# First block in another order: W1's product by inner halves, the low-rank rows turned in halves, GpSimd's splits elsewhere; in the last block the scores' shift ahead of a copy

## Chip, cores and metric

One core of a Trainium2 chip runs the whole program. The metric is the device time of one execution in microseconds (us).

## What is computed

x is 2 x 1024 x 256, the context 2 x 64 x 192, all float32. Four residual steps follow each other, each on a layer norm of x:

```
x = x + L0_xattn(_layernorm(x), ctx)   # 16 heads of 16; then relu(out @ W1 + b1) @ W2 + b2, W1 256 x 512
x = x + L0_ffn(_layernorm(x))          # for each of 8 experts: gate * (relu(x @ wi.T + bi + (x @ A_e.T) @ B_e.T) @ wo.T + bo)
x = x + L1_xattn(_layernorm(x), ctx)   # one head, width 256, softmax over 64 keys
x = x + L1_ffn(_layernorm(x))          # x @ weight.T + pooled @ disha
```

The gate of an expert is how often it is among the top two logits, times the sum of the two largest softmax values. So only two experts count for a row, and only their low-rank terms (A_e, B_e) differ.

## The kernel before

The 2048 rows are cut into 8 blocks of 256 rows (T = 256, two tiles of 128). Each block goes through stage a (first attention, W1, W2), stage f (experts), stage c (second attention and last product). The program writes out the order of each engine's work by hand: `opening()` is block 0's stage a and the start of its stage f together with all loads and weight preparation; `body(a, f, c, h)` runs seven times and mixes stage a of block a, stage f of block a-1, stage c of block a-2 and the queries of block a+1; `drain` and `end` finish the last two blocks. Engines are tied only by semaphores (`wait_ge`, `then_inc`).

Precision: most products are made three times in fp32r. Each operand is split in a high part (ScalarE copies the float32 value to fp32r) and a low part (VectorE or GpSimd subtracts the high part); the passes are high x high, low x high, high x low. Names end in _h and _l. For weights, `high_weights(n)` (ScalarE) and `low_weights(n)` (VectorE, counted in `lo_w`, or GpSimd, counted in `lo_wp`) do this once, in the opening: wq, w1, w2, wi in two halves, ga (A and the gate's weights, 128 x 272), lb (B), wo.

Names for the steps spoken of:
- `filler` (PE, L771): a product of zeros, used by nothing.
- `transposes(1, 0)` (L362) turn the normalised block 0; `values` (L685) are the first attention's values; `a_queries(0)` (L347) the queries; `a_row_scores` (L402) and `row_max` (VectorE, L1317) give each head's maximum; `first_scores` (L447), `first_exps` (ScalarE, L963), `first_attend` (L487, L488) the attention of block 0.
- `query_means` (L670, 4 products of float32) and a copy to `wqm` (VectorE, L1721): column means of Wq, used in block 1 and later.
- `a_hidden` (W1's product, into psS), ScalarE's `hidden` (relu, L1024) and `hidden_high` (L1029), `hidden_low` (GpSimd L1776 for the first half, VectorE L1665 for the second), `a_out` (W2's product, into psP), VectorE's `first_residual` (xmid, L1365) and `norm_stats(2, 0)`, GpSimd's `scale(2, 0)` (rs, L1759: the inverse root), ScalarE's `normalise(2, 0)` (xn, L970), `transposes(2, 0)`, `f_gate` (ga), VectorE's `experts` (am: the masked low-rank rows), `f_lora_transposes` (L543), ScalarE's `lora_high`, VectorE's `lora_low` (at_l, L1407), `f_first` (L567).
- `fold_turn`, `fold_means` (L642, L651), `constant_parts`, `constant_row` (L693, L700), `values1` (L685), `folded_keys` (L723, L726): preparation of stage c and of the experts' constant.
- `indicators(b)` (GpSimd, L1885): one 16 x 1024 table of each batch entry; the second is used from block 4 on.
- Last block (`end`): `end_turn` (L733) turns a tile, `passes` (L347) make its scores and linear part in one bank, ScalarE's `linear_part` (L1106) copies the linear part out, VectorE (L1519) shifts and scales the scores, ScalarE (L1110) takes the exponentials.

## Time and profile before

| what | value |
|---|---|
| median of 3 runs | 309.53 us (309.51 to 312.08) |
| the profiled execution's own time | 309.51 us |
| its span, first to last instruction | 307.5 us |
| mean granted TensorE clock | 0.994 |
| PE, DVE, ACT, POOL busy | 293.0, 256.8, 172.6, 161.2 us |
| chain that ended last | PE 83%, DVE 8%, ACT 3%, DMA 2%, POOL 1% |

Engines: PE is the matrix engine, PEld its weight loads, DVE is VectorE, ACT ScalarE, POOL GpSimd, SP the engine that issues DMAs. A float32 product leaves two records on PE, an fp32r product one. Records of PE overlap by their modelled ends, so starts are compared with starts. "Idle before" names what the engine waited for.

### The profile page before, as it was taken

The numbers are of one execution on the slowest core, as the hardware profiler recorded it, in microseconds if no ns is written. First come the engines' busy times: TensorE is split into PE (matmuls) and PEld (weight loads), VectorE is DVE, ScalarE is ACT, GpSimd is POOL, SyncE is SP. The second block draws the span as 40 slices with busy tenths as digits, with TensorE's granted clock in tenths as the row PEclk, the third lists the DMA queues.
The fourth block names the chain that finished last, engine by engine and source line by source line (L and its number), as shares of the span: only waits on it lengthen the run. The fifth ranks groups of instructions, "written<-read, shape, count | busy, mean of one in ns | idle before, by whom it ended". The sixth has DMA issues, their size and how long they took to land.

```text
span 307.5 us, 6696 instructions
## 1 busy us (share of the span) xinstructions
PE 293.0 (95%) x2548; PEld 272.3 (89%) x2548; DVE 256.8 (84%) x706; ACT 172.6 (56%) x359; POOL 161.2 (52%) x156
## 2 busy tenths in 40 slices
PE   7789998999999999999999999999999999999972
PEld 5559887999989998999999998999899998999971
DVE  3798988979899988998799889988899879755666
ACT  3548388564667267535846565826853584434521
POOL 2845665894085705581476318560659044803562
PEclk9999999999999999999999999999999999999997
DMA  7993320014021320133013301122023000000001
GB/s 234 395 388 105 73 68 2 0 45 128 2 19 39 71 100 2 24 89 114 2 19 77 96 35 19 44 71 91 3 29 94 36 0 2 0 36 1 2 34 34
DMA packets 15903, 20.18 MB, mean 66 GB/s; under 512 B 2912, under 2 KB 11872, under 8 KB 15616
## 3 DMA queue, kind: packets, MB, share of 16 engines
q1 hardware_dynamic: 14176, 16.19, 19.3%
q10 hardware_dynamic: 1696, 3.57, 3.2%
q8 instruction: 20, 0.33, 0.5%
q14 instruction: 11, 0.09, 0.2%
HBM read 11.62 MB, written 2.63 MB: 46 GB/s over the span
## 4 chain that ended last, share of the span: by engine, by line
PE 83%; DVE 8%; ACT 3%; DMA 2%; issue 2%; POOL 1%; SPq 0%; POOLq 0%; DVEq 0%
PE psI L567 13%; PE psP L347 13%; PE psI L338 12%; PE psI L347 12%; PE psS L347 7%; PE psT L338 4%; PE psP L502 2%; DMA kv<-in_kv 2%; PE psS L475 2%; PE psT L634 2%; PE psT L362 2%; PE psP L742 1%; PE psT L605 1%; PE psP L543 1%; ACT hs L1024 1%
## 5 line engine op out<-in xcount | busy, mean ns | idle before, releaser
L1759 POOL TENSOR_TENSOR rs<-ve,mhalf 128x2 f32<-128x2 f32 x30 | 22.0, 733 | 86.0 <-DVE ve L1285 86.0
L1782 POOL TENSOR_TENSOR hid_l<-r,hid_h 128x512 fp32r<-128x512 f32 x32 | 40.9, 1291 | 16.0 <-ACT hid_h L1049 16.0
L567 PE MATMUL psI<-at_h,lb_h 128*128 128x256 f32 x120 | 34.6, 289 | 0.8 <-DVE at_l L1407 0.8
L567 PE MATMUL psI<-at_h,lb_l 128*128 128x256 f32 x120 | 33.9, 282 | 0.0
L567 PE MATMUL psI<-at_l,lb_h 128*128 128x256 f32 x120 | 33.7, 281 | 0.0
L1415 DVE SCALAR_TENSOR_TENSOR r<-psI,nbi,r 128x256 f32<-128x256 f32 x60 | 26.1, 477 | 6.4 <-PE psI L567 6.4
L1776 POOL TENSOR_TENSOR hs_l<-hs,hs_h 128x512 fp32r<-128x512 f32 x15 | 19.6, 1310 | 20.6 <-ACT hs_h L1029 19.7
L970 ACT ACTIVATE xn<-xmid,nmr,rs 128x256 f32<-128x256 f32 x16 | 8.8, 595 | 35.8 <-POOL nmr L1763 35.8
L1044 ACT ACTIVATE r<-psI,first 128x256 f32<-128x256 f32 x60 | 25.0, 472 | 4.3 <-PE psI L567 4.3
L567 PEld LDWEIGHTS psI<-at_h,lb_h 128*128 128x128 f32 x120 | 22.6, 188 | 4.3 <-ACT r L1044 2.9
L1049 ACT ACTIVATE hid_h<-r 128x512 fp32r<-128x512 f32 x32 | 20.0, 628 | 11.0 <-DVE r L1415 10.8
L338 PE MATMUL psI<-xtf_h,wi_h 128*128 128x256 f32 x120 | 26.0, 298 | 0.0
L338 PE MATMUL psI<-xtf_h,wi_l 128*128 128x256 f32 x120 | 24.1, 283 | 0.0
L338 PE MATMUL psI<-xtf_l,wi_h 128*128 128x256 f32 x120 | 24.0, 282 | 0.0
L1008 ACT ACTIVATE ex<-psS 128x512 f32<-128x512 f32 x28 | 15.9, 599 | 13.6 <-PE psS L475 13.6
L567 PEld LDWEIGHTS psI<-at_h,lb_l 128*128 128x128 f32 x120 | 22.6, 189 | 0.0
L567 PEld LDWEIGHTS psI<-at_l,lb_h 128*128 128x128 f32 x120 | 22.6, 188 | 0.0
L338 PEld LDWEIGHTS psI<-xtf_h,wi_h 128*128 128x128 f32 x120 | 18.4, 189 | 2.2 <-issue 2.2
L338 PEld LDWEIGHTS psI<-xtf_l,wi_h 128*128 128x128 f32 x120 | 18.5, 189 | 0.0
L338 PEld LDWEIGHTS psI<-xtf_h,wi_l 128*128 128x128 f32 x120 | 18.5, 189 | 0.0
L1018 ACT ACTIVATE oa_h<-o 128x256 fp32r<-128x256 f32 x16 | 6.7, 418 | 18.2 <-DVE o L1358 17.3
L1767 POOL TENSOR_TENSOR oa_l<-o,oa_h 128x256 fp32r<-128x256 f32 x15 | 11.9, 809 | 9.4 <-ACT oa_h L1018 9.4
(344 smaller groups left out, 910.8 us busy)
## 6 DMA issues: line engine op xcount, KB each, us to landing
stack<-qu_h SPq DMA_DIRECT2D x56, 64.0 KB, 2.1
xin<-in_x SPq DMA_DIRECT2D x8, 256.0 KB, 2.8
stack<-qu_l SPq DMA_DIRECT2D x28, 64.0 KB, 2.0
out<-x ACTq DMA_DIRECT2D x7, 256.0 KB, 2.0
xn<-in_xt SPq DMA_DIRECT2D x5, 256.0 KB, 3.0
raw_w<-in_w ACTq DMA_DIRECT2D x2, 512.0 KB, 8.4
raw_wi<-in_wi SPq DMA_DIRECT2D x1, 1024.0 KB, 9.6
raw_wo<-in_wo SPq DMA_DIRECT2D x1, 1024.0 KB, 12.4
```

Source lines behind the costliest of these rows:

```text
L338: last = mm(out, lhs(a, c), rhs(b, c), start=start and q == 0 and k == 0, stop=stop and q == 2 and k == n - 1, **kw)
L347: last = mm(out, lhs(a, c), rhs(b, c), start=start and (a, b) == pairs[0] and i == 0 and k == 0, stop=stop and k == len(chunks) - 1, skip_ ...
L567: last = mm(bank[:, k * T:(k + 1) * T], (WH, WL)[x]["lb"][:, 0, f * P:(f + 1) * P], AT[y][:, which, :], start=False, stop=q == 2, skip_gro ...
L970: A(XN[j][:, t, :], src[:, t, :], ACT.Identity, scale=lnst[j][4][:, t:t + 1], bias=lnst[j][5][:, t:t + 1]).then_inc(S(f"ln{j}_xh"), 1)
L1008: A(EX[:, 2 * d:2 * d + 2, :], S_(d % 2).rearrange("p (k n) -> p k n", k=2), ACT.Exp, scale=SCALE).then_inc(S("ex"), 1)
L1044: last = A(R1[:, f, :], bank[:, k * T:(k + 1) * T], ACT.Relu, bias=cols[:, BI + f:BI + f + 1])
L1049: A(HH[:, 2 * u:2 * u + 2, :], R1[:, 2 * u:2 * u + 2, :], ACT.Identity).then_inc(S("hidh"), 1)
L1415: last = V.scalar_tensor_tensor(out=R1[:, f, :], in0=bank[:, k * T:(k + 1) * T], scalar=nbi[:, f:f + 1], in1=R1[:, f, :], op0=MAX, op1=ADD)
L1759: G_.tensor_tensor(rs[:, :], ve[:, :], mhalf[:, :], ALU.pow).then_inc(S(f"ln{j}_rs"), 1)
L1767: G_.tensor_tensor(OA[1][:, m, :], O32[:, m, :], as32(OA[0][:, m, :]), ALU.subtract).then_inc(S("ol"), 1)
L1776: G_.tensor_tensor(HS[1][:, two, :], HS32[:, two, :], as32(HS[0][:, two, :]), ALU.subtract).then_inc(S("hsl"), 1)
L1782: G_.tensor_tensor(HL[:, two, :], R1[:, two, :], as32(HH[:, two, :]), ALU.subtract).then_inc(S("hidl"), 1)
```

## The change

In `opening` PE makes the queries' means in two halves between products of block 0 and no longer after the attention, into another bank; four fillers more stand in it, at other places; the transposes of block 0 stand ahead of the values. W1's product of block 0 (`first_hidden`) takes the first inner half (m = 0) of all four output parts, then `values1(0)`, then the second inner half, so that it starts on the first half of the attention's output. Row scores of block 1 take the small form of later blocks. The queries of block 1 go to psP and no longer to psI, `constant_parts` move ahead and to psP, `fold_turn` and `fold_means` into the first body behind `f_first(0, 0)`. The low-rank rows of block 0 are turned, split and used in two halves. In the first body the low pass of `f_out(0, 0)` stands ahead of the next block's transposes. The small splits ga_l and wo_l change engine or place, `indicators(1)` moves to the second body with f = 1, the copy to gnum is gone from all blocks. In `end` the second tile's turn stands between the first tile's passes, the shift waits for the product and not for the copy, and the copies stand behind the exponentials.

PE, the first 13 us of the program, before and now (zeros is a filler, a_60 the keys, kv_61 the values, wq,avg the means, kb,qu_h the row scores):

```order
L678 MATMUL psI<-a_60 128x128 x4
L685 MATMUL psS<-kv_61 128x256 x2
L362 MATMUL psT<-first,xn 128x128 x4
L771 MATMUL psP<-zeros 128x256 x2
L347 MATMUL psP<-xta_h,wq_h 128x256 x4
L347 MATMUL psP<-xta_h,wq_l 128x256 x4
L347 MATMUL psP<-xta_l,wq_h 128x256 x4
L771 MATMUL psP<-zeros 128x256
L402 MATMUL psS<-kb,qu_h 128x512 x2
```

```order
L709 MATMUL psI<-a_60 128x128 x4
L802 MATMUL psP<-zeros 128x256 x3
L362 MATMUL psT<-first,xn 128x128 x4
L716 MATMUL psS<-kv_61 128x256 x2
L347 MATMUL psP<-xta_h,wq_h 128x256 x4
L347 MATMUL psP<-xta_h,wq_l 128x256 x4
L347 MATMUL psP<-xta_l,wq_h 128x256 x4
L700 MATMUL psT<-wq_h,avg 128x256 x2
L398 MATMUL psS<-kb,qu_h 128x512 x2
L398 MATMUL psI<-kb,qu_h 128x512 x2
L700 MATMUL psT<-wq_l,avg 128x256 x2
L802 MATMUL psP<-zeros 128x256
```

The means stand on both sides of the row scores, and the transposes stand ahead of the values.

PE, from the end of block 0's attention to block 1's queries, before and now (oa_h and oa_l are the attention's output, w_h and w_l are W1, xta the next block's input):

```order
L670 MATMUL psS<-wq_h,avg 128x256 x2
L670 MATMUL psS<-wq_l,avg 128x256 x2
L362 MATMUL psI<-first,xn 128x128 x4
L685 MATMUL psT<-kv_61 128x256 x2
L707 MATMUL psT<-a_60,kv_62 128x128 x4
L347 MATMUL psS<-oa_h,w_h 128x256 x4
L347 MATMUL psS<-oa_h,w_l 128x256 x4
L347 MATMUL psS<-oa_l,w_h 128x256 x4
L347 MATMUL psS<-oa_h,w_h 128x256 x4
L347 MATMUL psS<-oa_h,w_l 128x256 x4
L347 MATMUL psS<-oa_l,w_h 128x256 x4
L347 MATMUL psI<-xta_h,wq_h 128x256 x4
```

```order
L716 MATMUL psT<-kv_61 128x256 x2
L802 MATMUL psI<-zeros 128x256
L362 MATMUL psI<-first,xn 128x128 x4
L740 MATMUL psT<-a_60,kv_62 128x128 x4
L347 MATMUL psS<-oa_h,w_h 128x256 x2
L347 MATMUL psS<-oa_h,w_l 128x256 x2
L347 MATMUL psS<-oa_h,w_h 128x256 x2
L347 MATMUL psS<-oa_h,w_l 128x256 x2
L347 MATMUL psS<-oa_l,w_h 128x256 x4
L716 MATMUL psI<-kv_62,kv_61 128x256 x2
L347 MATMUL psS<-oa_h,w_h 128x256 x2
```

The means are gone here, and W1's product, 24 instructions in both, now has 12 on the first inner half, the values of the second attention, and 12 on the second inner half.

GpSimd from W1's product on, before and now (hsl counts finished low halves of the hidden values, rs is the inverse root):

```order
L1767 TENSOR_TENSOR oa_l<-o,oa_h 128x256 [waits oh]
L1892 TENSOR_TENSOR kb<-kt_h,first 128x512 [waits kt0_h]
L1892 TENSOR_TENSOR kb<-kt_h,first 128x512
L1776 TENSOR_TENSOR hs_l<-hs_59,hs_h 128x512 [waits hsh]
L1882 TENSOR_TENSOR wi_l<-raw_wi,wi_h 128x1024 [waits hi_w]
L1759 TENSOR_TENSOR rs<-ve,mhalf 128x2 [waits ln2_ve]
L1763 TENSOR_TENSOR nmr<-nm,rs 128x2 [waits ln2_rs]
L1799 TENSOR_TENSOR xr<-xin_50,kept 128x512 [waits x_in,x1]
L1882 TENSOR_TENSOR lb_l<-raw_lb,lb_h 128x1024 [waits hi_w]
L1922 TENSOR_TENSOR gw<-gw,late 128x2x256 [waits ld_late,ld_wc]
L1882 TENSOR_TENSOR wo_l<-raw_wo,wo_h 128x1024 [waits hi_w]
```

```order
L1825 TENSOR_TENSOR oa_l<-o,oa_h 128x256 [waits oh]
L1834 TENSOR_TENSOR hs_l<-hs_59,hs_h 128x512 [waits hsh]
L1946 TENSOR_TENSOR wi_l<-raw_wi,wi_h 128x1024 [waits hi_w,hsl]
L1946 TENSOR_TENSOR ga_l<-raw_ga,ga_h 128x272 [waits hi_w]
L1817 TENSOR_TENSOR rs<-ve,mhalf 128x2 [waits ln2_ve]
L1821 TENSOR_TENSOR nmr<-nm,rs 128x2 [waits ln2_rs]
L1955 TENSOR_TENSOR kb<-kt_h,first 128x512 x2
L1946 TENSOR_TENSOR lb_l<-raw_lb,lb_h 128x1024 [waits hi_w]
L1857 TENSOR_TENSOR xr<-xin_50,kept 128x512 [waits x_in,x1]
L1986 TENSOR_TENSOR gw<-gw,late 128x2x256 [waits ld_late,ld_wc]
L1817 TENSOR_TENSOR rs<-ve,mhalf 128x2 [waits ln1_ve]
L1821 TENSOR_TENSOR nmr<-nm,rs 128x2 [waits ln1_rs]
```

The table kb and lb_l stand behind block 0's rs now, ga_l (VectorE's before) ahead of it, and wo_l behind block 2's rs.

```diff
+            def first_hidden():
+
+                pe.wait_ge(S("lo_w"), 2)
+                parts = [[(S_(u)[:, k * T:(k + 1) * T], w("w1", (2 * u + k) * P), x_of(OA)) for k in range(2)]
+                         for u in range(NDH)]
+                for m in range(KC):
+                    pe.wait_ge(S("oh"), m + 1)
+                    for u in range(NDH):
+                        passes(parts[u], [m], ((0, 0), (1, 0)), m == 0, False)
+                    pe.wait_ge(S("ol"), m + 1)
+                    for u in range(NDH):
+                        last = passes(parts[u], [m], ((0, 1),), False, m == KC - 1)
+                        if m == KC - 1:
+                            last.then_inc(S("hs_ps"), 1)
+                    if m == 0:
+                        values1(0)
+
...
-                end_turn(b, 1)
...
+                def upper(t):
                     pe.wait_ge(S("ln3_h"), b + t + 1)
-                    passes(parts, range(KC), ((0, 0), (0, 1)), True, False)
+                    passes([(SCORES[t][:, 0:SY], x_of(XTC, t * P, P), folded_weights(b))], range(KC), ((0, 0), (0, 1)),
+                           True, False)
+
+                def lower(t):
                     pe.wait_ge(S("ln3_l"), b + t + 1)
-                    passes(parts, range(KC), ((1, 0),), False, True).then_inc(S("sc1_ps"), 1)
+                    passes([(SCORES[t][:, 0:SY], x_of(XTC, t * P, P), folded_weights(b))], range(KC), ((1, 0),),
+                           False, True).then_inc(S("sc1_ps"), 1)
+
+                upper(0)
+                end_turn(b, 1)
+                lower(0)
+                upper(1)
+                lower(1)
...
-                if A_:
-                    a_scores(a, 0)
-                    a_scores(a, 1)
-                if F_:
+                if f == 0:
+                    first_lora_transposes(0)
+                    first_lora_transposes(1)
+                a_scores(a, 0)
+                a_scores(a, 1)
+                if f > 0:
                     f_lora_transposes(f)
-                if f == 0:
-                    fold_means()
                 if C_:
                     c_scores(c, 0)
                     c_scores(c, 1)
                 if F_:
                     f_first(f, 0)
+                    if f == 0:
+                        fold_turn()
+                        fold_means()
                     if A_:
                         a_scores(a, 2)
                     f_first(f, 1)
@@ -867,7 +910,7 @@
                     a_row_scores(h, 1)
                 if F_:
                     f_out(f, 1, low=False)
-                if F_ and C_:
+                if F_:
                     f_out(f, 0, high=False)
...
-                if F_ and not C_:
-                    f_out(f, 0, high=False)
...
+                pe.wait_ge(S("ld_first"), 16)
+                filler(P_(1), 3)
+                transposes(1, 0, T_(1))
                 pe.wait_ge(S("ld_kv0"), 16)
                 values(S_(0)[:, 0:D], kv0, 0).then_inc(S("v0_ps"), 1)
-                pe.wait_ge(S("ld_first"), 16)
-                transposes(1, 0, T_(1))
-                filler(P_(1), 2)
                 a_queries(0)
-                filler(P_(1), 1)
+                query_means(0)
                 pe.wait_ge(S("v0"), 1)
                 a_row_scores(0, 0)
                 pe.wait_ge(S("kt0_l"), KC)
                 a_row_scores(0, 1, I_)
+                query_means(1)
+                filler(P_(1), 1)
                 first_scores(((0, 0), (1, 0)))
                 first_max_transposes()
                 first_scores(((0, 1),))
                 first_scores_less_maxima()
+                filler(I_(1), 2)
                 first_attend(0)
                 first_attend(1)
-                query_means()
+                values(T_(1)[:, 0:D], kv0, 1).then_inc(S("v0_ps"), 1)
+                filler(I_(1), 1)
                 transposes(1, 1, I_(0))
-                values(T_(1)[:, 0:D], kv0, 1).then_inc(S("v0_ps"), 1)
                 keys1()
-                a_hidden(0, 0)
-                pe.wait_ge(S("centred"), 2)
-                a_hidden(0, 1)
-                a_queries(1, I_(1))
+                first_hidden()
+                a_queries(1)
                 a_out(0, 0)
                 a_out(0, 1)
-                pe.wait_ge(S("kt1"), 1)
-                pe.wait_ge(S("v0"), BATCH)
-                a_row_scores(1, 0, T_)
-                a_row_scores(1, 1, S_)
-                values1()
+                row_scores(1)
+                constant_parts()
+                values1(1)
                 folded_keys()
                 pe.wait_ge(S("mx"), 2 * NT - 1)
                 transposes(2, 0, T_(1))
-                pe.wait_ge(S("mx"), 2 * NT)
-                constant_parts()
+                folded_biases()
                 a_max_transposes(1)
+                pe.wait_ge(S("crow"), 1)
                 f_gate(0, 1)
+                constant_row()
                 pe.wait_ge(S("gb"), 1)
                 f_base(0, 0)
-                constant_row()
                 pe.wait_ge(S("v1"), 1)
                 f_base(0, 1)
-                fold_turn()
...
                 def linear_part(t):
-                    act.wait_ge(S("sc1_ps"), b * NT + t + 1)
+                    act.wait_ge(S("sc1b"), b * NT + t + 1)
                     A(YB[b // BPB][:, t, :], SCORES[t][:, at:at + D], ACT.Identity).then_inc(S("y"), 1)
 
                 def weights(t):
@@ -1117,12 +1160,12 @@
                 for t in range(NT):
                     tile_high(3, b, t, XTC)
                 store(b - 1)
-                linear_part(0)
-                linear_part(1)
                 weights(0)
                 turned(0)
                 weights(1)
                 turned(1)
+                linear_part(0)
+                linear_part(1)
...
+                act.wait_ge(S("centred"), 1)
+                A(wqm[:, :], T_(0)[:, 0:D], ACT.Identity).then_inc(S("centred"), 1)
                 first_maxima()
                 first_exps(0)
                 first_exps(1)
                 normalise(1, 1, x_of_block(1))
                 attended(0, 0)
+                high(1, 1, XTA, I_(0))
                 high_weights("wi", 0, 2)
-                high(1, 1, XTA, I_(0))
                 attended(0, 1)
...
+                high_weights("wo")
+                act.wait_ge(S("crow_ps"), 1)
+                A(y[:, 0:D], P_(0)[:, 0:D], ACT.Identity).then_inc(S("crow"), 1)
                 normalise(2, 0, XMID)
                 high(2, 0, XTF, T_(1))
-                act.wait_ge(S("crow_ps"), 1)
-                A(y[:, 0:D], S_(1)[:, 0:D], ACT.Identity).then_inc(S("crow"), 1)
...
-                high_weights("wo")
...
-                V.tensor_copy(gnum[:, :], lg3[:, :, 0])
...
-                    dve.wait_ge(S("y"), b * NT + t + 1)
+                    dve.wait_ge(S("sc1_ps"), b * NT + t + 1)
...
-                if F_:
+                if f == 0:
+                    first_lora_low(0)
+                    constant()
+                    first_lora_low(1)
+                    gates(0)
+                    dve.wait_ge(S("nbi"), 1)
+                else:
                     lora_low(f)
...
@@ -1698,46 +1761,41 @@
...
+                low(1, 0, XTA, T_(1))
...
-                low(1, 0, XTA, T_(1))
+                masked_values(0, S_(0))
                 dve.wait_ge(S("kt0_l"), KC)
                 diagonal(kd_l, kt0_l, "kd_l")
-                dve.wait_ge(S("ld_vrows"), 16)
-                first_values(0, S_(0)[:, 0:D])
                 row_max(0, 0)
                 row_max(0, 1, psI)
                 queries_low(0)
-                low_weights("w1")
+                first_values(0)
                 dve.wait_ge(S("x_in"), 32)
                 dve.wait_ge(S("ln1_xh"), NT)
                 norm_stats(1, 1, x_of_block(1))
+                low_weights("w1")
                 V.tensor_scalar(nbi[:, :], cols[:, BI:BI + NFF], -1.0, None, MULT).then_inc(S("nbi"), 1)
                 first_attended(0)
                 first_attended(1)
-                dve.wait_ge(S("centred"), 1)
-                V.tensor_copy(wqm[:, :], S_(1)[:, 0:D]).then_inc(S("centred"), 1)
                 attended_low(0, 1)
                 low(1, 1, XTA, I_(0))
-                first_values(1, T_(1)[:, 0:D])
+                low_weights("wi", 1, 2)
+                masked_values(1, T_(1))
+                first_values(1)
                 keys_of_second()
-                low_weights("wi", 1, 2)
                 hidden_low(0, 1)
                 queries_low(1)
-                low_weights("ga")
                 first_residual(0)
                 dve.wait_ge(S("x1"), 1)
                 norm_stats(2, 0, XMID)
-                row_max(1, 0, psT)
-                row_max(1, 1)
+                heads_max(1, 1, psT)
+                heads_max(1, 0, psS)
+                values_of_second()
                 low(2, 0, XTF, T_(1))
-                values_of_second()
                 experts(0)
-                constant()
...
+                if f == 0:
+                    low_weights("wo", 0, 2)
...
+                if f == 1:
+                    pool.wait_ge(S("ol"), (a + 1) * KC)
+                    indicators(1)
+                    pool.wait_ge(S("tables"), 4)
...
@@ -1902,26 +1965,26 @@
                 pool.wait_ge(S("ld_first"), 16)
                 pool.wait_ge(S("ln1_nmr"), 1)
                 indicators(0)
-                indicators(1)
+                pool.wait_ge(S("tables"), 1)
                 pool.wait_ge(S("ld_vrows"), 16)
                 G_.tensor_copy(heads[:, :], heads32).then_inc(S("tables"), 1)
-                low_weights("w2", 0, 1)
                 pool.wait_ge(S("ld_kept"), 16)
                 residual(0)
+                low_weights("w2", 0, 1)
                 scale(1, 1)
                 attended_low(0, 0)
-                pool.wait_ge(S("kt0_h"), KC)
+                hidden_low(0, 0)
+                pool.wait_ge(S("hsl"), NDH)
+                low_weights("wi", 0, 2)
+                low_weights("ga", 0, 1)
+                scale(2, 0)
                 second_row_keys()
-                hidden_low(0, 0)
-                low_weights("wi", 0, 2)
-                scale(2, 0)
+                low_weights("lb", 0, 1)
                 residual(1)
-                low_weights("lb", 0, 1)
                 pool.wait_ge(S("ld_wc"), 16)
                 pool.wait_ge(S("ld_late"), 16)
                 G_.tensor_tensor(GWR[:, :, KEYS:KEYS + D], GWR[:, :, KEYS:KEYS + D],
                                  late[:, D:2 * D].unsqueeze(1).broadcast_to([P, KC, D]), ALU.add).then_inc(S("wc_sum"), 1)
-                low_weights("wo", 0, 2)
```

## Rows read from the trace of the kernel before

**Rows 1.** Windows view, columns as named in its head (us; PEclk of 1.00 full).

```profile
0.00:20.00 20.00, 14.38 (x106) 10.68 (x108) 13.10 (x32) 8.75 (x18) 10.91 (x11) 1.00 0.93 332
20.00:60.00 40.00, 38.87 (x330) 34.33 (x323) 34.68 (x77) 27.55 (x55) 23.92 (x22) 1.00 0.26 77
60.00:290.00 230.00, 229.58 (x2056) 218.82 (x2055) 196.86 (x557) 132.16 (x279) 117.40 (x114) 1.00 0.18 43
290.00:307.50 17.50, 10.15 (x69) 8.44 (x67) 12.17 (x42) 4.09 (x11) 8.96 (x11) 0.89 0.08 30
```

**Rows 2.** PE timeline to 22 us: start, duration, engine, line, operation, tiles, records, idle before.

```profile
4.89 2.05 PE L678 MATMUL psI<-a 96*128 96x128 f32 x8
8.50 1.13 PE L685 MATMUL psS<-kv 96*128 96x256 f32 x4 [1.56 <-DMA kv<-in_kv]
...
12.34 0.59 PE L771 MATMUL psP<-zeros 128*128 128x256 f32 x2
13.47 0.70 PE L402 MATMUL psS<-kb,qu_h 128*128 128x512 f32 x2 [0.54 <-issue]
...
15.49 0.39 PE L447 MATMUL psS<-qu_h,kd_h 32*128 32x256 f32 x2 [0.85 <-DVE mx L1317]
...
19.27 0.63 PE L487 MATMUL psP<-ex,v0z 128*32 128x256 f32 x4 [0.84 <-ACT ex L963]
```

**Rows 3.** DVE timeline to 25 us.

```profile
17.27 1.81 DVE L1638 TENSOR_TENSOR w_l<-raw_w,w_h 128x1024 fp32r<-128x1024 f32 x1
...
20.86 1.76 DVE L1329 RECIPROCAL rec<-psP 128x256 f32<-128x256 f32 x1 [0.49 <-PE psP L488]
```

**Rows 4.** PE timeline, 20 to 73 us.

```profile
21.84 1.13 PE L670 MATMUL psS<-wq_h,avg 128*128 128x256 f32 x4
...
32.07 1.11 PE L347 MATMUL psP<-w_h,hs_l 128*128 128x256 f32 x8
...
37.51 0.84 PE L362 MATMUL psT<-first,xn 128*128 128x128 f32 x4 [0.33 <-ACT xn L970]
...
40.27 0.61 PE L347 MATMUL psP<-ga_h,xtf_l 128*128 128x136 f32 x4
...
47.63 0.36 PE L567 MATMUL psI<-at_h,lb_h 128*128 128x256 f32 x1 [0.79 <-DVE at_l L1407]
...
50.43 1.09 PE L502 MATMUL psP<-ex,v 64*32 64x256 f32 x32
...
72.31 0.93 PE L362 MATMUL psT<-first,xn 128*128 128x128 f32 x4
```

**Rows 5.** ACT timeline around W1's product.

```profile
29.81 0.63 ACT L1029 ACTIVATE hs_h<-hs 128x512 fp32r<-128x512 f32 x1
```

**Rows 6.** DVE timeline, 32 to 45 us.

```profile
32.03 1.72 DVE L1638 TENSOR_TENSOR ga_l<-raw_ga,ga_h 128x272 fp32r<-128x272 f32 x1
33.67 0.68 DVE L1365 TENSOR_TENSOR xmid<-psP,xr 128x512 f32<-128x512 f32 x1
...
44.73 2.15 DVE L1403 TENSOR_TENSOR gate<-gnum,grec 128x2 f32<-128x2 f32 x1
```

**Rows 7.** GpSimd (POOL) timeline, first block.

```profile
7.26 5.62 POOL L1885 TENSOR_SCALAR ks<-first 16x1024 fp32r<-16x1024 f32 x2 [0.17 <-POOL nmr L1763]
...
30.59 2.85 POOL L1882 TENSOR_TENSOR wi_l<-raw_wi,wi_h 128x1024 fp32r<-128x1024 f32 x1
35.77 0.69 POOL L1759 TENSOR_TENSOR rs<-ve,mhalf 128x2 f32<-128x2 f32 x1 [2.32 <-DVE ve L1285]
```

**Rows 8.** GpSimd timeline, third body.

```profile
93.17 1.60 POOL L1767 TENSOR_TENSOR oa_l<-o,oa_h 128x256 fp32r<-128x256 f32 x2 [0.81 <-ACT oa_h L1018]
97.65 2.73 POOL L1776 TENSOR_TENSOR hs_l<-hs,hs_h 128x512 fp32r<-128x512 f32 x2 [2.88 <-ACT hs_h L1029]
```

**Rows 9.** ACT timeline in the last block.

```profile
298.53 0.38 ACT L1106 ACTIVATE y<-psS 128x256 f32<-128x256 f32 x1 [0.50 <-PE psS L347]
298.81 0.34 ACT L1110 ACTIVATE sc<-sc,mx 128x64 f32<-128x64 f32 x1
```

128 lines of the change are left out of this document (75 added, 53 removed).

## The prediction

> **What bounds the kernel now.** I read the windows first. PE is busy 229.6 of 230 us between 60 and 290, so seven blocks stand on PE's own work, and the change leaves their lists nearly as they are: time can come only from the first 60 us and the last 17.5 [rows 1]. In 0 to 20 PE is idle 5.6 us, in 20 to 60 only 1.1, at the end 7.4 [rows 1]. Then the chain of waits and the timelines of that stretch, engine by engine. The waits that PE shows after 20 us are 0.33 before block 0's second transposes (37.51) and 0.79 before its low-rank products (47.63) [rows 4]. All else that the opening can give is PE work taken out of a full stretch and put into a hole. The reader is to look for three things: holes before 20 us (0.54, 0.85 and 0.84 long) [rows 2], the chain through VectorE and GpSimd to the inverse root rs at 35.77 [rows 6, 7], and the place that a moved step finds in its new queue.
>
> **To 20 us.** Block 0's transposes now go ahead of the values (1.13 busy) and of two fillers (0.5 each by the row at 12.34) [rows 2]. Three fillers stand before them. The keys' eight records of 128 columns take 2.05, 0.26 each, and just after, four records of 256 columns take 1.13, 0.28 each: half the pace per column first, though the granted clock reads 1.00 for the whole window [rows 1, 2]. So keys ran at the lower level (1.2 GHz), values at the upper (2.4). Three fillers cost 1.5 at the upper, 3.0 at the lower level, from 6.94 on; the transposes then start between 8.5 and 9.9, against 9.46 before. I take 0.7 earlier for the queries (ends 0 and 0.9).
>
> Half of the means then fills the hole before the row scores at 13.47, in place of a filler. The other half (1.13) and a filler (0.5) stand in a hole of 0.85 before 15.49 [rows 2, 4]: 0.7 too much, less the half us by which VectorE's maxima also come earlier. Two more fillers (1.0) stand in a hole of 0.84 before 19.27 [rows 2]: 0.15 too much. Of the 0.7 there is 0.35 left at the attention (ends -0.3 and 0.9). VectorE's reciprocal at 20.86 waited 0.49 for PE; ahead of it there is now also the value bias (0.9), while w_l, 1.81 long, was partly blocked; I take the reciprocal 0.3 earlier [rows 3].
>
> **20 us to the hidden values.** The means, two rows of 1.13, some 2.0, leave PE here; a filler (0.5) comes, and one of the two values products (0.9) comes in the middle of W1's product [rows 2, 4]. W1's product needs 24 x 0.12 = 2.9 us. Its first half can start on the first half of the attention, some 2 us earlier than before, but its last half still ends after values and 12 products: hs_ps for both output halves comes at about 27.6 and 27.8. Before, the first came near 27.4, the second near 28.8. ScalarE's relu and copy then run in a row either way, and hs_h, whose last ended at 30.44 [rows 5], ends at 30.5. So of the product by inner halves **nothing** arrives at W2; the work of 1 us that PE saves is paid as a wait of 0.4 there and as queries made earlier. W2's last pass started at 32.07 and ended at 33.18; I take 32.5, 0.6 earlier, since its first half no longer queues behind the queries [rows 4].
>
> **To rs and the gate.** VectorE's xmid started only at 33.67 although W2 was ready at 33.18, because ga_l, 1.72 long from 32.03, stood in front [rows 4, 6]. ga_l is gone from there: xmid at 32.5, 1.15 earlier. Statistics follow in 2.1 us (33.67 to rs at 35.77), so rs could start at 34.6. GpSimd now has wi_l and ga_l ahead of it: wi_l waits for VectorE's hs_l, 31.2, takes 2.4 to 2.85 (the row at 30.59), and ga_l, a quarter of its width, 0.7 [rows 7]: free at 34.6 to 34.8. I take rs at 34.85: **0.9 gained**. Transposes start at 36.6, f_gate's last pass at 39.15 instead of 40.27 [rows 4]: 1.1, since the constant's products no longer stand behind the transposes.
>
> ScalarE now has wo_h (1.9 us) in front of xn; it ends near 34.5 and y near 34.9, and xn is due at 35.85: hidden with 1 us to spare, and if the cover goes it costs what it lacks.
>
> **Gate to the first body.** The copy to gnum goes, the low-rank rows come in halves, so the first half is turned before VectorE makes the rest. Before, PE waited 0.79 for at_l, after gate (2.15 us for 128x2) had held VectorE [rows 4, 6]; now at_l of the first half waits for transposes, scores and ScalarE only, 0.25 of wait. fold_turn and fold_means, 1.8 together, are moved behind f_first and change nothing in the sum. 1.1 + 0.54: **1.65 us** at the first attention of block 1 (50.43 before, 48.8 now) [rows 4]. Row scores in the small form stream as many columns as the wide ones; I count them equal.
>
> **First body and end.** The transposes at 72.31 take 0.93 because they stand on the second xn, a third of it waiting; a low pass of the experts' output now fills this: 0.3 [rows 4]. wo_l (2.4 to 2.85) is now in the first body of GpSimd, indicators(1) in the second, where GpSimd idled 2.88 before hs_l; one table costs half of 5.62, 2.81 [rows 7, 8]. It just fits: 0. In the last block the copy y, 0.38 long, stood before the exponential at 298.81 [rows 9]. Both go, but the second turn is 0.25 later on PE, and VectorE's shift comes after a low part that is as much later: 0.25 gained (ends 0 and 0.5). Taken out of the other blocks is only the gnum copy, on an engine that doesn't bound them.
>
> **Sum**: 1.65 + 0.3 + 0.25 = 2.2, from the profiled execution's 309.51, which is the median of the runs to 0.02: 307.3, and with the small row scores, counted equal and hardly dearer, I say **307.2**. By the ends of the terms 305.2 to 309.2.
>
> **Rivals.**
> *GpSimd's two splits hold rs.* ga_l on VectorE took 1.72 for 272 columns, while GpSimd ran wi_l until 33.44, and it ended 0.31 after that [rows 6, 7]: the two seem to exclude each other. If ga_l on GpSimd takes 1.72 too and wi_l 2.85 from 31.2, GpSimd is free at 35.8, and nm on VectorE waits behind it: rs at 36.1, later than before. That takes 1.2 off the 2.2: 308.5. Chance 0.2. The Trainium skill, page "SBUF — State Buffer", section "Who interferes with whom", says that a VectorE instruction with two SBUF inputs and a GpSimd instruction that reads SBUF exclude each other for a whole instruction; by that rule, with which the row at 32.03 agrees, the splits moved to GpSimd free VectorE's list but not its port.
>
> *All holes are filled.* If the start keeps its 0.9 and the wait for hs_h vanishes, the opening gives 2.0 of means, the two waits (0.33, 0.79) and 0.9, less a filler 0.5, 3.5, with 0.5 for body and end: 305.5. Chance 0.17. For it: PE has almost no other bound after 20 us. Against: the ScalarE chain at 29.81 [rows 5].
>
> *GpSimd becomes the bound (slower).* In the first body wo_l comes in (up to 2.85), in the second indicators(1) (2.81), each ahead of splits that PE waits for. The slot in the second has 0.07 to spare [rows 8]. If neither finds its slot, W2 of blocks 1 and 2 waits 5.7: 309.5 - 2.2 + 5.7 = 313.0. It decides as soon as hs_l in the second body starts over 0.3 later after oa_l than the table's own length. Against: GpSimd is busy only 117 of 230 us [rows 1]. Chance 0.05, most of it between 310 and 313.
>
> **Numbers.** A measurement tells about 1% from nothing, 3.1 us here. The forecast (0.58) covers 306.1 to 308.1, the full holes 305.0 to 306.1, the splits 308.1 to 309.3, GpSimd's bound above. The range 305.2 to 309.2 leaves some 2 in 10 out. Below 306.4 lie the 0.17 and a quarter of the forecast: faster 0.32; above 312.6 some 0.03; same 0.65.
>
> **What would show it.** Right: rs of block 0 near 34.9, f_gate's last pass near 39.1, the first attention of block 1 near 48.8, no PE wait over 0.3 behind 40 us, the same block pace up to 290, the exponential 0.25 earlier against the last products. Wrong: hs_h ending well before 30.4 (inner halves do arrive), rs at 36, an idle before W2's last pass in blocks 1 or 2, the attention of block 0 later than 19.27.

## The result and the profile after

The changed kernel takes 309.03 us, the median of 21 runs (308.59 to 310.89, and one of 1590.74 left aside), the kernel before 311.4, the median of 21 runs (309.51 to 316.23). The ratio is 0.9935, with a 95% interval of 0.9914 to 0.9955; executions over 1.5% above the fastest of the same kernel are left out of every ratio. The forecast of 307.2 stood against the profiled execution of the kernel before, 309.51. The profiled execution after is 309.13 (span 306.9), so the change gave **0.38 of the 2.2 us** that the sum promised. Beside it stands an effect of which the sum knew nothing: the kernel before needs 1 to 6.7 us more in most of its other executions, the changed one in one of 20. So the medians are 2.37 apart and 309.03 lies inside the range that I gave, but both are luck: nearly all of that distance comes from this effect and not from the terms of the sum.

The windows view of the kernel after, columns as in [rows 1]:

```profile
0.00:20.00 20.00, 17.54 (x128) 12.74 (x130) 14.41 (x35) 9.80 (x21) 9.80 (x11) 1.00 0.93 324
20.00:60.00 40.00, 38.46 (x333) 33.57 (x327) 31.88 (x72) 27.65 (x54) 24.41 (x23) 1.00 0.27 81
60.00:290.00 230.00, 229.01 (x2052) 218.68 (x2050) 196.30 (x551) 132.01 (x277) 119.87 (x115) 1.00 0.18 43
290.00:306.90 16.90, 10.20 (x66) 8.23 (x64) 11.74 (x41) 3.69 (x11) 8.66 (x11) 0.85 0.09 31
```

To be seen: PE is 3.2 us busier before 20 us, with fillers and means; between 60 and 290 it has 0.6 us less of busy time, a wait that was not there before.

PE timeline of the kernel after; the rows that answer to [rows 2, 4] (start, duration, engine, line, operation, tiles, records, idle before):

```profile
18.76 0.73 PE L486 MATMUL psP<-ex,v0z 128*32 128x256 f32 x6
...
31.61 1.10 PE L347 MATMUL psP<-w_h,hs_l 128*128 128x256 f32 x8
...
36.60 0.84 PE L362 MATMUL psT<-first,xn 128*128 128x128 f32 x4 [0.34 <-ACT xn L1009]
...
39.14 0.61 PE L347 MATMUL psP<-ga_h,xtf_l 128*128 128x136 f32 x4
...
43.37 0.44 PE L561 MATMUL psP<-first,am 128*128 128x128 f32 x2 [0.28 <-DVE am L1434]
44.34 0.44 PE L561 MATMUL psP<-first,am 128*128 128x128 f32 x2 [0.54 <-DVE am L1438]
...
49.63 1.09 PE L501 MATMUL psP<-ex,v 64*32 64x256 f32 x32
...
72.40 0.60 PE L362 MATMUL psT<-first,xn 128*128 128x128 f32 x4
...
75.89 0.63 PE L634 MATMUL psT<-first,x 128*128 128x128 f32 x4 [0.57 <-DVE x L1474]
```

Up to f_gate's last pass nearly all came as forecast: block 0's attention 0.51 earlier, W2's last pass 0.46 (its end at 32.71, forecast 32.5), the second transposes 0.91, f_gate 1.13 (39.14 against the forecast's 39.15). Then 0.33 is lost up to block 1's attention (49.63, 0.80 earlier than in [rows 4] and not 1.65), and at 72.40 the transposes start later than before, though the second xn, on which they stand, started 0.80 earlier (70.86 against 71.66). A new wait of 0.57 stands before the turn at 75.89, which started at 76.28 in the kernel before: 0.39.

Counted from the start of block 0's attention, the turn comes after 57.13 in the changed kernel and after 57.01 in the kernel before. So behind the attention the new order gave nothing up to here, and all of the 0.39 was there before 20 us. Even that is not shown to be the change's: in another execution of the kernel before (run 13 below, 309.31 us) the attention started as early as in the changed one.

```profile
18.75 0.63 PE L487 MATMUL psP<-ex,v0z 128*32 128x256 f32 x4 [0.85 <-ACT ex L963]
```

VectorE's and GpSimd's timelines of the kernel after, from xmid to the place where 0.85 of the promised 1.65 is missing:

```profile
32.74 0.69 DVE L1412 TENSOR_TENSOR xmid<-psP,xr 128x512 f32<-128x512 f32 x1 [0.60 <-PE psP L347]
...
40.27 1.16 DVE L1425 TENSOR_TENSOR srtd<-srt 128x16 f32<-128x16 f32 x1
...
41.75 0.92 DVE L1430 CAST idxf<-idx 128x16 f32<-128x16 uint32 x1
```

```profile
34.86 0.69 POOL L1817 TENSOR_TENSOR rs<-ve,mhalf 128x2 f32<-128x2 f32 x1 [0.35 <-DVE ve L1333]
...
35.78 2.05 POOL L1955 TENSOR_TENSOR kb<-kt_h,first 128x512 fp32r<-128x512 f32 x2
37.78 2.37 POOL L1946 TENSOR_TENSOR lb_l<-raw_lb,lb_h 128x1024 fp32r<-128x1024 f32 x1
40.10 1.30 POOL L1857 TENSOR_TENSOR xr<-xin,kept 128x512 f32<-128x512 f32 x1
41.34 1.30 POOL L1986 TENSOR_TENSOR gw<-gw,late 128x512 f32<-128x512 f32 x1
```

VectorE's xmid and GpSimd's rs answer to [rows 6, 7]: 0.93 and 0.91 earlier, forecast 1.15 and 0.92. But two tiny VectorE operations on 128x16, a difference (40.27) and a cast (41.75), take 1.16 and 0.92 us. The first ends just as GpSimd's xr ends (41.40), the second just as its gw ends (42.64).

### The profile page after: what moved, and what is told of

It reads as the page before. It is cut to its first block, busy times and chain, and to the rows that moved or that the text cites. A ratio compares the mean times of both kernels' runs of the same rounds, so it can differ in the third digit from the quotient of the medians.

```text
span 306.9 us, 6740 instructions
## 1 busy us (share of the span) xinstructions
PE 295.2 (96%) x2568; PEld 273.2 (89%) x2568; DVE 254.3 (83%) x697; ACT 173.2 (56%) x361; POOL 162.7 (53%) x157
## 4 chain that ended last, share of the span: by engine, by line
PE 83%; DVE 8%; ACT 4%; DMA 1%; issue 1%; POOL 1%; POOLq 0%; DVEq 0%
PE psI L592 13%; PE psP L347 13%; PE psI L347 13%; PE psI L338 12%; PE psS L347 7%; PE psT L338 4%; PE psP L501 2%; PE psS L474 2%; PE psT L663 2%; PE psT L362 2%; DMA xin<-in_x 1%; PE psP L774 1%; PE psT L634 1%; PE psP L568 1%; ACT hs L1063 1%
## 5 line engine op out<-in xcount | busy, mean ns | idle before, releaser
L1817 POOL TENSOR_TENSOR rs<-ve,mhalf 128x2 f32<-128x2 f32 x30 | 23.0, 765 | 88.2 <-DVE ve L1333 88.2
L1009 ACT ACTIVATE xn<-xmid,nmr,rs 128x256 f32<-128x256 f32 x16 | 8.8, 596 | 32.5 <-POOL nmr L1821 32.5
```

The source lines that it names most:

```text
L1009: A(XN[j][:, t, :], src[:, t, :], ACT.Identity, scale=lnst[j][4][:, t:t + 1], bias=lnst[j][5][:, t:t + 1]).then_inc(S(f"ln{j}_xh"), 1)
L1817: G_.tensor_tensor(rs[:, :], ve[:, :], mhalf[:, :], ALU.pow).then_inc(S(f"ln{j}_rs"), 1)
```

## The experiments

**1. The low pass put back.** Repair of the turn:

```diff
-                if F_:
+                if F_ and C_:
                     f_out(f, 0, high=False)
...
                     transposes(2, a, T_(1))
+                if F_ and not C_:
+                    f_out(f, 0, high=False)
                 if F_:
                     f_out(f, 1, high=False)
```

> In the first body the low pass of the experts' output of tile 0 goes back behind the second transposes of block 1; nothing else differs from the changed kernel. Theory (the pass is on the way): the changed kernel reached the turn of the first body only 0.39 us earlier than the kernel before, though all up to the transposes was 0.8 earlier; the order before lets the transposes and VectorE's x2 start while the pass runs, so the second turn comes 0.3 to 0.5 earlier and the time is 308.6 to 308.8 (from 309.0 to 309.1). Rival (the place does not matter, VectorE's own chain from the residual on sets the turn): 309.0 to 309.1, turn unchanged at 75.9. My prediction's step said the opposite, that the new place gains 0.3: then this kernel takes 309.3 to 309.4.

Measured: 308.32 (308.16 to 308.51). PE timeline of this run, then VectorE's:

```profile
71.44 0.93 PE L362 MATMUL psT<-first,xn 128*128 128x128 f32 x4
...
75.41 0.61 PE L634 MATMUL psT<-first,x 128*128 128x128 f32 x4
```

```profile
74.31 0.87 DVE L1476 SCALAR_TENSOR_TENSOR x<-psI,gate,xg 128x256 f32<-128x256 f32 x2
```

The two executions do not start their first attention at the same time, so I count from it (18.76 in the changed kernel, 18.63 here): the turn comes after 56.78 instead of 57.13, 0.35 less, and its wait is gone. The transposes now wait on the second xn again (0.93 for 0.60), but VectorE's x, which the turn needs, follows the transposes by its own chain of splits: it started at 74.88 and now at 74.31. The time says 0.7; up to the turn the trace bears out half of that. 0.13 more came before the attention, and no row tells where the rest, some 0.2 behind the turn, was gained.

**2, 3. GpSimd taken away from VectorE's expert rows**, in two ways. Second row keys early:

```diff
                 attended_low(0, 0)
+                pool.wait_ge(S("kt0_h"), KC)
+                second_row_keys()
                 hidden_low(0, 0)
...
                 scale(2, 0)
-                second_row_keys()
                 low_weights("lb", 0, 1)
```

> GpSimd makes the second row keys right behind the low half of the attention, in its idle of 5.5 us, as before the change; the split of lb, the residual for block 1 and the sum on the means' weights then run some 2 us earlier and end before VectorE's expert rows start. Theory (GpSimd's long SBUF operations hold VectorE's small ones): VectorE's difference of sorted logits and its cast of indices, 1.16 and 0.92 long in the changed kernel, take under 0.25 each, am starts 1.5 us earlier, the attention of block 1 starts near 48.9 instead of 49.6, and the time is 308.3 to 308.6. Rival (those records wait for ScalarE or for PE): they stay near 1 us, the attention stays at 49.6, 309.0 to 309.1. Second rival: the keys land on W2's weights split (w2) or the low half of hidden and delay W2: attention of block 1 later than 49.6, 309.3 or more.

Or residual and sum late, the keys left where they are:

```diff
                 low_weights("lb", 0, 1)
+                pool.wait_ge(S("am"), 1)
                 residual(1)
```

> The second row keys stay where the changed kernel has them, but GpSimd waits for VectorE's masked products to be complete before the residual of block 1 and the sum on the means' weights. Theory (those two operations hold VectorE): the difference of sorted logits and the cast take under 0.25 each as in the run with early keys, am starts 1.5 us earlier; the residual and the sum then run beside VectorE's first splits, so part is given back: attention of block 1 between 48.9 and 49.5, 308.4 to 308.9. Rival (the records' length has another cause): unchanged at 1.16 and 0.92, 309.0 to 309.2.

Measured: 308.19 (307.93 to 308.34) and 307.87 (307.76 to 308.15). VectorE's timeline, keys early, then residual late:

```profile
40.30 0.36 DVE L1425 TENSOR_TENSOR srtd<-srt 128x16 f32<-128x16 f32 x1
...
40.98 0.18 DVE L1430 CAST idxf<-idx 128x16 f32<-128x16 uint32 x1
```

```profile
39.71 0.17 DVE L1425 TENSOR_TENSOR srtd<-srt 128x16 f32<-128x16 f32 x1
...
40.20 0.17 DVE L1430 CAST idxf<-idx 128x16 f32<-128x16 uint32 x1
```

PE with the keys early:

```profile
44.43 0.36 PE L592 MATMUL psI<-at_h,lb_h 128*128 128x256 f32 x1 [0.42 <-DVE at_l L1453]
...
48.94 1.09 PE L501 MATMUL psP<-ex,v 64*32 64x256 f32 x32
```

The same difference takes 0.36 and 0.17, the cast 0.18 and 0.17. With the keys early gw runs from 39.37 to 40.63 and still touches the difference; with the residual late nothing of GpSimd runs there. From block 0's attention to block 1's it is 30.17 and 30.18, against 30.87: **0.7 us** by either way. The rivals fall: the operations waited neither for ScalarE nor for PE. "Part is given back" in the third run is refuted too. The Trainium skill, page "SBUF — State Buffer", section "Who interferes with whom", says that a VectorE instruction with two SBUF inputs, or a copy or cast that uses two ports, and a GpSimd instruction that reads SBUF exclude each other for a whole instruction; the trace agrees, for both kinds.

**4. W1 in the plain order** (its inner halves undone):

```diff
-                first_hidden()
+                pe.wait_ge(S("lo_w"), 2)
+                a_hidden(0, 0)
+                a_hidden(0, 1)
+                values1(0)
```

> W1's product of block 0 runs in the plain order again (first all of output half 0, then all of half 1), with the values of the second attention behind it; the rest is the changed kernel. Theory (ScalarE's chain relu and copies ends W2's wait anyway): the last split of the hidden values moves by less than 0.3, W2's second half waits as before, 309.0 to 309.3. Rival (the inner halves do arrive at W2): PE waits for the second half of the attention ahead of W1, up to 1.5 us, and later marks move by 0.8 to 1.5: 309.8 to 310.5.

Measured: 309.46 (309.25 to 309.98). PE timeline:

```profile
25.29 0.71 PE L347 MATMUL psS<-oa_h,w_h 128*128 128x256 f32 x4 [1.13 <-ACT oa_h L1060]
...
32.43 1.11 PE L347 MATMUL psP<-w_h,hs_l 128*128 128x256 f32 x8
```

PE waits 1.13 for the second half of the attention, and W2's last pass starts 13.59 after block 0's attention instead of 12.85. So 0.74 does arrive at W2, more than the theory allowed and less than the rival's range in time. ScalarE's last hs_h ended at 29.93 here and at 30.50 in the changed kernel, 0.57 earlier where the theory allowed 0.3: in this order ScalarE is not the end of the chain, PE is, since queries and W2 come behind the hole. That the halves give nothing at hs_h was right; that they give nothing at W2 was wrong for this kernel. The kernel before, in the plain order and with the means in that place, reached W2's last pass after 12.80, so the halves only fill the hole that the moved means left.

**5, 6, 9, 10. Fillers**, to find why the kernel before scatters. Holes of the kernel before filled, except the one behind the keys:

```diff
-                filler(P_(1), 1)
+                filler(P_(1), 2)
                 pe.wait_ge(S("v0"), 1)
                 a_row_scores(0, 0)
                 pe.wait_ge(S("kt0_l"), KC)
                 a_row_scores(0, 1, I_)
+                filler(P_(1), 2)
...
                 first_scores_less_maxima()
+                filler(I_(1), 2)
```

> The kernel before, with one filler more (two products of 128x256 on zeros) ahead of the row scores of block 0, two behind them and two ahead of the first attention, so that PE's holes of 0.54, 0.85 and 0.84 us before 20 us are full; they change no result. The kernel before ran at 309.5 to 316 with a mean granted clock down to 0.974 in its longer runs, the changed one at 308.6 to 309.4 at 0.991 to 0.996. Theory (the holes of the opening let the granted clock fall in some executions, and what the change gained in the median is mostly this): this kernel runs at 309.5 to 310.3 with under 0.5 of scatter, clock 0.991 or more in every run. Rival (the scatter comes from something after 20 us that the change moved, or from when the program is started): 309.5 to 316 as before, median near 311.5. Cost of the fillers themselves: 0 to 0.5.

The changed kernel without its seven fillers:

```diff
                 keys0()
                 pe.wait_ge(S("ld_first"), 16)
-                filler(P_(1), 3)
...
                 query_means(1)
-                filler(P_(1), 1)
...
-                filler(I_(1), 2)
                 first_attend(0)
...
-                filler(I_(1), 1)
                 transposes(1, 1, I_(0))
```

> The changed kernel without its seven fillers behind the keys (3 ahead of the transposes, 1 behind the second half of the means, 2 ahead of the attention, 1 ahead of block 1's transposes). Theory (holes let the clock fall in some executions): runs scatter from 308.5 to 314, some at a clock of 0.98 or less. Rival (the fillers are for nothing, PE would be waiting there): all runs between 308.0 and 309.2, clock 0.99 or more; where a filler stood on the way, up to 0.5 is gained.

Measured: 311.01 (308.96 to 312.92; the kernel before 312.21 beside it) and 309.53 (308.24 to 310.57). The first refutes its theory: with the later holes full the scatter stays. The trace of the second shows the clock fall, windows view and PE:

```profile
5.00:10.00 5.00, 3.71 (x19) 2.98 (x19) 3.61 (x12) 3.25 (x7) 3.63 (x3) 0.97 1.01 337
10.00:15.00 5.00, 5.00 (x23) 4.54 (x22) 4.21 (x6) 2.42 (x4) 3.21 (x4) 0.69 1.05 405
15.00:20.00 5.00, 3.36 (x59) 2.17 (x61) 4.90 (x13) 2.17 (x8) 2.25 (x2) 1.00 1.00 385
```

```profile
8.01 0.84 PE L362 MATMUL psT<-first,xn 128*128 128x128 f32 x4 [1.29 <-ACT xn L1005]
...
9.62 1.09 PE L347 MATMUL psP<-xta_h,wq_h 128*128 128x256 f32 x4
```

Behind the keys PE was idle for 1.29, then the granted clock fell to 0.69 in 10 to 15 us, and four records of the queries took 1.09 instead of 0.71. So the next two runs test the hole behind the keys alone, from both sides. Three fillers in the kernel before:

```diff
                 keys0()
+                filler(P_(1), 3)
                 pe.wait_ge(S("ld_kv0"), 16)
```

> The kernel before with one edit: three fillers (six products on zeros, 1.5 us) right behind the keys of block 0, where PE otherwise waits for the values' transfer. In the run without the change's fillers PE was idle for 1.29 us at that place and the granted clock then read 0.69 from 10 to 15 us. Theory (the one hole behind the keys lets the clock fall, in most executions of the kernel before): runs at 309.0 to 309.8, clock 0.99 or more in nearly all, ratio to before 0.990 to 0.994. Rival (it takes all the fillers, or the later holes): 309 to 314 still, median 311 or more. Second rival (the fillers themselves stand on the way): all runs tight but at 310 to 311.

and the changed kernel without the same three:

```diff
                 pe.wait_ge(S("ld_first"), 16)
-                filler(P_(1), 3)
                 transposes(1, 0, T_(1))
```

> The changed kernel with only the three fillers behind the keys taken out; the other four stay. Theory (this hole decides): like the run without any filler, most executions at 309.3 to 310.5 with a clock of 0.993 down to 0.985, one or another near 308.7. Rival (the later fillers hold the clock up): all at 308.6 to 309.3.

Measured: 309.27 (308.99 to 311.28), ratio to the kernel before 0.9947 (0.9918 to 0.9975), and 309.88 (309.1 to 311.53). Both theories hold in the main: the three fillers bring the kernel before from 311.76 to 309.27 (from 311.3 where its six executions over 314 are left out), and without them the changed kernel loses 0.85 in the median. But it then still stands 1.9 below the kernel before, so the fillers are not the only part of the change that takes the scatter away; which other part does is not shown. The trace of this last run kept its level behind a hole of 1.29; what its other executions did is seen in their times alone. Two of twelve runs with the fillers still took 311.2 to 311.3.

**13 to 16. The kernel before again**, four more traces:

> The kernel before, unchanged, for one more trace of it. Theory (the hole behind the keys lets the granted clock fall in most executions): where the time is over 310 us, the granted clock reads clearly under 1.00 for some us between 8 and 20 us, the products in it run at half their pace, and from 30 us on each mark is later by the same amount. Rival (the loss is elsewhere): the opening is as in the trace already shown and the time goes between 30 and 300 us.

> The kernel before again, for another trace: the same two readings.

> The kernel before again, for another trace: the same two readings.

> The kernel before again, for another trace: the same two readings.

Measured: 309.31, 312.21, 312.02 and 310.51. The third, windows and PE:

```profile
5.00:10.00 5.00, 3.12 (x13) 2.47 (x14) 4.56 (x12) 2.24 (x5) 3.35 (x3) 0.77 1.04 368
10.00:15.00 5.00, 5.00 (x22) 4.64 (x21) 2.99 (x7) 1.54 (x2) 3.48 (x3) 0.55 1.04 401
15.00:20.00 5.00, 3.21 (x46) 1.90 (x45) 3.30 (x5) 1.91 (x4) 3.11 (x2) 1.00 1.01 393
60.00:290.00 230.00, 229.52 (x2051) 218.96 (x2051) 197.61 (x558) 133.12 (x281) 117.31 (x114) 1.00 0.17 43
```

```profile
5.18 1.16 PE L678 MATMUL psI<-a 96*128 96x128 f32 x8 [0.41 <-DMA a<-in_a]
8.04 2.08 PE L685 MATMUL psS<-kv 96*128 96x256 f32 x4 [1.70 <-DMA kv<-in_kv]
...
12.11 1.42 PE L347 MATMUL psP<-xta_h,wq_h 128*128 128x256 f32 x4
...
15.96 0.70 PE L402 MATMUL psS<-kb,qu_h 128*128 128x512 f32 x2 [0.54 <-issue]
...
52.92 1.09 PE L502 MATMUL psP<-ex,v 64*32 64x256 f32 x32
```

The keys ran at the upper level (1.16; 2.05 in [rows 2]), PE then waited 1.70 for the transfer of the values, and the granted clock fell to 0.55 of full in 10 to 15 us, which is the lower level (1.2 GHz) for most of it. The values take 2.08 and not the 1.13 of [rows 2], the queries' four records 1.42 and not 0.71. The row scores start at 15.96 against 13.47: 2.49 late; block 1's attention at 52.92 against 50.43: still 2.49. The whole loss is in the opening. The fourth trace shows the same at half the size (1.64 idle, then 0.80 and 0.86 granted). The first, with 1.10 idle, lost nothing. The second lost 2.28 up to the row scores, but in another way:

```profile
5.03 2.08 PE L678 MATMUL psI<-a 96*128 96x128 f32 x8
7.95 2.08 PE L685 MATMUL psS<-kv 96*128 96x256 f32 x4 [0.84 <-DMA kv<-in_kv]
```

Its values took 2.08 behind 0.84 of idle time, and its keys ahead of that had taken 2.08 too. So here no fall is seen: PE was at the lower level before the hole and stayed there until about 14 us (the queries' last pass, from 14.09, took 0.68), while every other trace shows the upper level somewhere before 9 us. Its windows read 1.00 all the same, as they do beside the slow keys of [rows 2]: there the pace shows the level and the clock column does not.

**7. Both repairs together**, the edits of 1 and 2:

> The changed kernel with both repairs: the low pass of tile 0 behind the second transposes in the first body, and the second row keys early on GpSimd. Each alone gave 308.32 and 308.19 against 309.03. Theory (the two losses are apart, one at the gate and one at the turn): the gains add, 0.7 + 0.84 by the times, 0.70 + 0.34 by the marks in the traces: 307.5 to 308.0, attention of block 1 at 0.7 and the first body's turn at 1.0 less than the changed kernel's after the start of block 0's attention. Rival (the turn waits for one chain of VectorE that either repair frees): 308.1 to 308.3.

Measured: 307.72 (307.47 to 308.31). From block 0's attention (18.39) block 1's comes after 30.17 and the turn (74.42) after 56.03, against 57.13: 1.10 less, the sum of 0.70 and 0.35 to 0.05. They add, as the theory had it.

**8. The last block as before**, in the changed kernel: end_turn(b, 1) back in the drain, the copies y ahead of the exponentials:

```diff
-                    act.wait_ge(S("sc1b"), b * NT + t + 1)
+                    act.wait_ge(S("sc1_ps"), b * NT + t + 1)
...
+                linear_part(0)
+                linear_part(1)
                 weights(0)
...
-                    dve.wait_ge(S("sc1_ps"), b * NT + t + 1)
+                    dve.wait_ge(S("y"), b * NT + t + 1)
```

> The changed kernel with the last block as before: the second turn behind the low products of tile 1 at once, the copies y ahead of the exponentials and VectorE's shift behind the copies. Theory (prediction's term): the end costs 0.25 more, 309.2 to 309.4, the last exponential 0.25 later against the second products. Rival (the end is set by VectorE's shift and maxima, which do not wait for the copies): 309.0 to 309.1. Rival (the turn on PE cost more than the copy): 308.8 to 308.9.

Measured: 309.41 (308.89 to 311.03), 0.38 more. ACT timeline of the changed kernel, then of this one; its first exponential against [rows 9]:

```profile
298.12 0.35 ACT L1153 ACTIVATE sc<-sc,mx 128x64 f32<-128x64 f32 x1 [0.94 <-DVE mx L1574]
```

```profile
298.26 0.34 ACT L1153 ACTIVATE sc<-sc,mx 128x64 f32<-128x64 f32 x1
```

From PE's last low products (294.96 and 294.67) the exponential starts after 3.16 and after 3.59, and VectorE's last x ends after 9.77 and 10.15. The end is worth **0.38**, a little over the 0.25 I gave it.

**11. ga's split back on VectorE:**

```diff
                 queries_low(1)
+                low_weights("ga")
                 first_residual(0)
```

(GpSimd's goes, and the waits count accordingly.)

> The changed kernel with the split of ga back on VectorE, between the low half of the second queries and the residual; GpSimd goes from the split of wi straight to the inverse root. Theory (prediction's step: ga_l stood in front of xmid): VectorE's ga_l is held by GpSimd's wi_l until 33.8, xmid starts at 33.9 to 34.0 instead of 32.74, rs at 36.0, the gate 1.1 later, 309.9 to 310.2. Rival (xmid was late for W2): xmid within 0.3 of 32.74, 309.0 to 309.3.

Measured: 310.32 (309.54 to 313.2). VectorE, then GpSimd:

```profile
31.96 2.02 DVE L1695 TENSOR_TENSOR ga_l<-raw_ga,ga_h 128x272 fp32r<-128x272 f32 x1
33.90 0.68 DVE L1412 TENSOR_TENSOR xmid<-psP,xr 128x512 f32<-128x512 f32 x1
```

```profile
31.28 2.39 POOL L1947 TENSOR_TENSOR wi_l<-raw_wi,wi_h 128x1024 fp32r<-128x1024 f32 x1 [0.90 <-DVE hs_l L1728]
36.00 0.69 POOL L1818 TENSOR_TENSOR rs<-ve,mhalf 128x2 f32<-128x2 f32 x1 [2.32 <-DVE ve L1333]
```

ga_l takes 2.02 for 272 columns and ends 0.31 after GpSimd's wi_l; xmid starts at 33.90 and rs at 36.00, 1.16 and 1.14 later than in the changed kernel. This bears out the step of the prediction (xmid 1.15 earlier without it). The median is 1.29 above the changed kernel's, but four of the twelve executions took 311.95 to 313.2 at a mean granted clock of 0.981 or 0.982, with all fillers in place. None of them was traced, so the 1.16 and 1.14 are the better measure, and the scatter can come back by a way that is open.

**12. The turn in the wait for at_l**, on top of both repairs:

```diff
-                    first_lora_low(0)
                     constant()
+                    first_lora_low(0)
...
+                    if f == 0:
+                        fold_turn()
                     f_first(f, 0)
                     if f == 0:
-                        fold_turn()
                         fold_means()
```

> The kernel with both repairs (307.72) and one edit more: VectorE makes the constant row in its idle time of 1.08 us ahead of the first low half of the low-rank rows, and PE turns the folded values (0.43 busy) ahead of the first low-rank product instead of behind it, where it waited 0.42 for at_l. Theory (the wait is filled and the work leaves the way): the wait is under 0.1, attention of block 1 0.3 to 0.4 earlier, 307.3 to 307.5. Rival (the constant's place delays at_l by its 0.41, or the turn waits for the constant): 307.7 to 308.1.

Measured: 307.35 (four runs 307.22 to 307.38, two at 308.4 and 309.1). PE:

```profile
43.62 0.60 PE L671 MATMUL psT<-first,v 128*128 128x128 f32 x4
44.20 0.36 PE L592 MATMUL psI<-at_h,lb_h 128*128 128x256 f32 x1
...
48.28 1.09 PE L501 MATMUL psP<-ex,v 64*32 64x256 f32 x32
```

No wait stands before the first low-rank product, and block 1's attention comes 29.73 after block 0's, against 30.17. This is the fastest kernel: 1.7 less than the changed one.

## Why the prediction was wrong, step by step

The sum said 2.2 against 309.51; 0.38 came.

- **To 20 us**: 0.51 against 0.35, but not shown to come from the change. The values' transfer lands at 7.95 to 8.50 in five executions of the kernel before, and the attention started at 18.75 in run 13 and at 18.73 in run 9, as early as the 18.76 here.
- **The hidden values**: W2 ended 0.2 later than I had it (xmid at 32.74, I said 32.5). The reason was half right: ScalarE's chain ended at 30.50 as forecast, but in the changed kernel the inner halves are worth 0.74 at W2 (run 4). "Nothing" holds only against the kernel before, where the means filled that place.
- **To rs and the gate**: right, 34.86 for 34.85 and 39.14 for 39.15, with the cause shown by run 11. The rival "GpSimd's two splits hold rs" is refuted: wi_l took 2.40 and ga_l 0.77, and GpSimd was free 0.35 before it was needed. The rival "all holes are filled" fell too: PE waited 0.34 for xn, and 0.28 and 0.54 for am.
- **Gate to the first body, "1.1 + 0.54"**: this term failed. I reckoned the wait for at_l to shrink from 0.79 to 0.25. In its place came 0.28 and 0.54 for am, because VectorE's difference and cast were held 1.73 us too long by GpSimd's xr and gw (runs 2 and 3 give 0.7 back), and with them away 0.42 for at_l (run 12 gives 0.44). I had listed what moves to GpSimd and asked only whether GpSimd would be done in time; I applied its exclusion with VectorE to 31 to 36 us and not to the operations that the late keys pushed to 40 to 42.6. Nothing there is late on GpSimd. What matters is what VectorE does meanwhile. The sign was in the trace of the kernel before: the 2.15 of gate on 128x2 [rows 6], which I took for gate's own length, ends at 46.88, just as GpSimd's wo_l of that kernel ends (46.87):

```profile
44.52 2.35 POOL L1882 TENSOR_TENSOR wo_l<-raw_wo,wo_h 128x1024 fp32r<-128x1024 f32 x1 [2.98 <-ACT wo_h L1083]
```

In the changed kernel wo_l runs later, and the same gate takes 0.16.
- **First body, "a low pass now fills this: 0.3"**: wrong in sign. The hole of 0.33 is filled, but the pass holds the transposes back, and with them VectorE's two splits and x, on which the turn stands: run 1 gives 0.35 back. The chain behind the hole had no slack, which the row at 72.31 did not tell me and VectorE's timeline behind it would have.
- **GpSimd's tables**: right; indicators(1) ran from 94.47 for 2.78, and PE waits for hs_l 0.2 once, as in the kernel before.
- **The end**: 0.38 for 0.25 (run 8), the best-sized of the small terms.
- **What the sum rests on**: one execution. The hole of 1.56 behind the keys [rows 2] I took as room and not as a risk; in three of the four further traces the products behind it ran at half pace, which cost 1.05 to 2.5 us, though in one of the three PE had been at the lower level before it. In the kernel before three fillers are worth 2.5 us in the median, 2.0 without its longest executions (run 9), and they bring it to 309.27, 0.24 above the changed kernel. In the changed kernel the same three are worth 0.85 (run 10), so these are not shares that add up. The longest executions of the kernel before, 314 to 316, were not traced; that the same hole makes them is argued only from the fillers. I weighed the fillers by the pace of the keys and never asked what the clock does behind a hole.

With the two failed terms repaired the kernel runs at 307.72, 1.8 under the 309.51 that I started from. The full 2.2 takes run 12 (307.35), whose edit is neither in the change nor in the forecast.

## To carry to other kernels

A step moved to GpSimd has two costs: whether it ends in time, and which small VectorE operations with two SBUF inputs (or copies) on the critical chain fall inside its duration; write down both. Before a hole on PE is filled with real work, follow the chain of what stands behind the hole; if VectorE or ScalarE start their own chain from it, the filling is paid there. Where the times of a kernel scatter, trace several executions before summing parts of a us, and look at the first hole behind the start: products on zeros that nobody needs may be the best part of a change.

## What was not expected of the hardware

- The granted clock falls back right after the start in an execution-dependent way: after 1.70 and 1.64 of idle time it fell (0.55 and 0.86 in 10 to 15 us), after 1.56 ([rows 2]) and 1.10 it did not, and after 1.29 it fell in run 6 and not in the trace of run 10. The length of the hole alone does not decide. In one further execution (run 14) PE was still at the lower level in the keys and left it only near 14 us. What decides either is open.
- A VectorE difference on 128x16 took 1.16 in place of 0.17 beside a GpSimd addition of 1.30 on 128x512: the small one ends with the large one, and here paid nearly all of it.
- The time outside the span was 1.9 to 2.1 in the kernels built on the kernel before and 2.2 to 2.3 in those built on the changed one, but 2.05 to 2.16 in run 11, which differs from it only in ga's split. So 0.2 of the span's gain of 0.6 does not reach the time; no run tells why.
